# Turning x one element ahead, with the attention product and the low keys on POOL

## The reference

```python
qkv = x @ Wqkv + bqkv                       # q: 16 heads of 16; k, v: 4 groups of 16, tiled to 16 heads
scores = einsum('bqhd,bkhd->bhqk', q, k) / HD
out = einsum('bhqk,bkhd->bqhd', softmax(scores), v)
x1 = layernorm(x + out @ Wout + bout)
gate, up = split(x1 @ ternary_quant(w_gate_up).T)     # H = 1024
h = silu(gate) * up
y = layernorm(x1 + rms_norm(h) @ ternary_quant(w_proj).T)
```

## Time and profile before

| | |
|---|---|
| median of three runs | 575.34 us |
| profiled execution | 574.5 us, span 571.8 us |
| PE busy | 528.4 us, 92% |
| DVE busy | 455.4 us, 80% |
| ACT busy | 374.2 us, 65% |
| POOL busy | 319.5 us, 56% |
| mean granted clock of TensorE | 0.990 |

### The profile page before, as it was taken

How to read it: one execution, slowest core, us unless ns; L and a number is a source line. 1 busy time by engine, 2 the same in 40 slices (tenths; PEclk the granted TensorE clock), 3 DMA queues, 4 the chain that set the end, 5 groups by cost and what they waited for, 6 DMA issues and landing times.

```text
span 571.8 us, 13792 instructions
## 1 busy us (share of the span) xinstructions
PE 528.4 (92%) x4176; PEld 444.7 (78%) x4176; DVE 455.4 (80%) x1025; ACT 374.2 (65%) x754; POOL 319.5 (56%) x478
## 2 busy tenths in 40 slices
PE   6497999999999999999999999999999999999883
PEld 5386778778888787878888888878887877787772
DVE  6878877788888888888888887888898888885764
ACT  5456755666767767676776776776767676667663
POOL 5577671255645555555646564556555565466764
PEclk9899999999999999999999999999999999999998
DMA  7865444343333426062534444261606253010001
GB/s 229 144 142 95 86 95 104 74 91 88 84 95 93 105 68 128 19 160 26 128 69 102 93 94 100 79 116 56 134 6 166 29 125 71 12 44 6 19 20 37
DMA packets 53931, 49.05 MB, mean 86 GB/s; under 512 B 6144, under 2 KB 53888, under 8 KB 53888
## 3 DMA queue, kind: packets, MB, share of 16 engines
q1 hardware_dynamic: 53200, 48.13, 38.2%
q10 hardware_dynamic: 688, 0.39, 0.2%
HBM read 33.29 MB, written 14.68 MB: 84 GB/s over the span
## 4 chain that ended last, share of the span: by engine, by line
PE 63%; DVE 20%; issue 7%; POOL 4%; ACT 2%; DMA 2%; SPq 0%; DVEq 0%; ACTq 0%; POOLq 0%
PE ffn_ps L551 19%; PE short_ps L477 10%; PE pv_ps L579 8%; PE short_ps L523 8%; PE down_ps L564 7%; PE exp_ps L532 6%; DVE row_max L800 5%; DVE gated L863 3%; DVE h_f L870 3%; PE short_ps L587 2%; DVE attB L902 2%; DVE pvT L896 1%; DVE w_hat L833 1%; POOL sq_sum L966 1%; DVE w_sum L821 1%
## 5 line engine op out<-in xcount | busy, mean ns | idle before, releaser
L800 DVE TENSOR_REDUCE row_max<-short_ps 128x2 f32<-128x512 f32 x256 | 173.4, 681 | 67.2 <-PE short_ps L523 66.8
L961 POOL TENSOR_TENSOR h_lo<-h_f,h_hi 128x256 fp32r<-128x256 f32 x128 | 94.8, 740 | 206.9 <-ACT h_hi L698 206.8
L722 ACT ACTIVATE probs<-exp_ps 128x1024 f32<-128x1024 f32 x128 | 130.7, 1021 | 34.1 <-PE exp_ps L532 33.2
L523 PE MATMUL short_ps<-k_st,q_st 65*128 65x256 f32 x512 | 108.2, 294 | 9.3 <-DVE v_ones L919 6.2
L523 PEld LDWEIGHTS short_ps<-k_st,q_st 65*128 65x128 f32 x512 | 87.9, 192 | 20.7 <-issue 7.8
L707 ACT ACTIVATE tanh<-ffn_ps 128x256 f32<-128x256 f32 x120 | 45.5, 380 | 85.2 <-PE ffn_ps L551 85.2
L551 PE MATMUL ffn_ps<-x1T_hi,wguT 128*128 128x256 f32 x480 | 82.0, 293 | 10.3 <-DVE h_f L870 8.9
L564 PE MATMUL down_ps<-wpT,h_hi 128*128 128x256 f32 x256 | 78.7, 330 | 3.8 <-POOL h_lo L961 3.8
L532 PE MATMUL exp_ps<-q_st,k_st 67*128 67x512 f32 x256 | 80.7, 397 | 0.8 <-DMA q_st<-shift_lo 0.6
L551 PEld LDWEIGHTS ffn_ps<-x1T_hi,wguT 128*128 128x128 f32 x480 | 64.8, 189 | 19.3 <-issue 9.7
L966 POOL TENSOR_TENSOR sq_sum<-sq_sum,h_sq 128x256 f32<-128x256 f32 x105 | 79.5, 758 | 0.0
(11 more groups left out here) (102 smaller groups left out, 830.7 us busy)
## 6 DMA issues: line engine op xcount, KB each, us to landing
q_st<-q_dram SPq DMA_DIRECT2D x128, 128.0 KB, 4.1
q_dram<-q_p SPq DMA_DIRECT2D x16, 512.0 KB, 3.0
xn<-in_L_attn_x_dram SPq DMA_DIRECT2D x16, 256.0 KB, 3.4
k_st<-k_dram SPq DMA_DIRECT2D x64, 64.0 KB, 2.8
res<-in_L_attn_x_dram SPq DMA_DIRECT2D x16, 256.0 KB, 2.9
out_dram<-y_out SPq DMA_DIRECT2D x16, 256.0 KB, 2.9
wgu_raw<-in_L_ffn_w_gate_up_dram SPq DMA_DIRECT2D x8, 256.0 KB, 6.6
k_dram<-k_p SPq DMA_DIRECT2D x16, 128.0 KB, 2.4
```

The source lines that it names most:

```text
L523: last = pe.matmul(bank[:, t * S:(t + 1) * S], q_st[0:PAD, st.par, head, t * P:(t + 1) * P], k_st[0:PAD, st.par, st.s % 4, :], start=True, ...
L722: act.activation(probs[:, st.s % 4], exp_ps[:], ACT.Exp).then_inc(exp_done, 1)
L800: dve.tensor_reduce(row_max[:, st.par, head * TT:(head + 1) * TT], short(n, f"max{i}")[:].rearrange("p (t k) -> p t k", t=TT), AX.X, ALU.m ...
L961: pool.tensor_tensor(h_p[1][:, st.s % 4, :], h_f[:, st.s % 2, :], h_p[0][:, st.s % 4, :].bitcast(F32), ALU.subtract).then_inc(h_lo, 1)
```

## The change

Four things are changed.

- **x**: it is loaded one element earlier (`LOAD_X = -8`) and turned at offset -2, that is in slot 6 of the element before, ahead of `down` and not behind it, and ACT's copy of it stands in slot 6 too. It uses bank `short2` and not `short0`. Element 0 is still turned in slot 1, element 1 in slot 6 of the ramp.
- **Attention product**: for elements 2 to 14 the multiplication (`attB`) is done by POOL, one slot later (slots 5 and 1) and first in POOL's slot; DVE's turning of it (`attT`) stands at the end of the same slots.
- **Low part of k**: from element 3 on POOL computes it, in slot 4, ahead of the second layer norm's small steps.
- **Identity products**: in slot 8 of the ramp PE does 18 more of them, behind a wait on the first piece's eviction (`w_ev`).

The loop starts at slot 72 and makes three passes instead of four.

```diff
-LOAD_X = 0
-X_T = 1
+LOAD_X = -8
+X_T = -2
+FIRST_X_T = 1
...
+PV_BACK = (21, 25)
...
-X_HIGH = 1
...
-              1: {"max0": 0, "max1": 2, "x": 0, "shift1": 1},
+              1: {"max0": 0, "max1": 2, "shift1": 1},
...
-              6: {"max0": 0, "max1": 1},
+              6: {"max0": 0, "max1": 1, "x": 2},
...
+CLOCK_WAIT, CLOCK_LONG = 8, 18
...
-LOOP_FROM, BODY = 64, 2 * SLOTS
+LOOP_FROM, BODY = 72, 2 * SLOTS
...
+def x_turn(n):
+
+    if n.it is None and n.t == FIRST_X_T:
+        return Step(0, 0, None)
+    st = n.once(X_T)
+    return st if st and (st.it is not None or st.b) else None
...
+def product_on_pool(st):
+
+    return st.it is not None or 2 <= st.b < B - 1
+
+
+def low_keys_on_pool(st):
+
+    return st.it is not None or st.b >= 3
...
+        def normalised(eng):
+            return eng.tensor_tensor(
+                attB[:].rearrange("p (b g d) -> p g b d", b=NB, g=2),
+                pvT[:].rearrange("p (g b e) -> p g b e", g=2, b=NB)[:, :, :, 0:HD],
+                den_r[:].rearrange("p (g b) -> p g b", g=2).unsqueeze(3).broadcast_to([P, 2, NB, HD]),
+                ALU.mult).then_inc(att_done, 1)
...
@@ block.tensor, slot
                 keep_clock(n, 2)
+                if st := x_turn(n):
+                    bank = short_ps[BANK[X_T % SLOTS, "x"]] if st.it is None and st.b == 0 else use_short(n, "x")
+                    if st.it is None and st.b == 1:
+                        pe.wait_ge(k_copied, 1)
+                    wait(pe, x_loaded[st.par], st.count2(16, 16))
+                    turn(bank, [xn[:, st.par, t, k * P:(k + 1) * P] for k in range(DT) for t in range(TT)], xT_made)
                 if st := n.chunk(DOWN0):
                     down(st)
-                if st := n.once(X_T):
-                    bank = use_short(n, "x")
-                    wait(pe, x_loaded[st.par], st.count2(16, 16))
-                    turn(bank, [xn[:, st.par, t, k * P:(k + 1) * P] for k in range(DT) for t in range(TT)], xT_made)
                 if (c := turned_piece(n, 0)) is not None:
                     turn_weights(c)
+                if n.it is None and n.t == CLOCK_WAIT:
+                    pe.wait_ge(w_ev, 1)
+                    for _ in range(CLOCK_LONG):
+                        pe.matmul(turn_banks[0][:, 0, 0:P], ident[:], ident[:], start=True, stop=True)
...
@@ block.scalar, slot
-                if st := n.once(X_HIGH):
+                if st := x_turn(n):
                     wait(act, xT_made, st.count(1, 1))
                     wait(act, k_made, st.count(1, 0))
                     high(xT[:], both(n, "x")).then_inc(xT_copied, 1)
...
@@ block.vector
+            def turn_attention(st, half):
+
+                wait(dve, att_done, st.count(2, half + 1))
+                wait(dve, o_made, st.count(1, 0))
+                dve.transpose(attT[:, half, :], attB[:]).then_inc(att_turned, 1)
...
-                        wait(dve, den_done, st.count(2, half + 1))
-                        wait(dve, att_turned, st.count(2, half))
-                        dve.tensor_tensor(
-                            attB[:].rearrange("p (b g d) -> p g b d", b=NB, g=2),
...
-                        wait(dve, att_done, st.count(2, half + 1))
-                        wait(dve, o_made, st.count(1, 0))
-                        dve.transpose(attT[:, half, :], attB[:]).then_inc(att_turned, 1)
-                if st := keys(n):
+                        if not product_on_pool(st):
+                            wait(dve, den_done, st.count(2, half + 1))
+                            wait(dve, att_turned, st.count(2, half))
+                            normalised(dve)
+                            turn_attention(st, half)
+                    if (st := n.once(PV_BACK[half])) and product_on_pool(st):
+                        turn_attention(st, half)
+                if (st := keys(n)) and not low_keys_on_pool(st):
                     wait(dve, k_copied, st.count(1, 1))
                     low(k_p[:, 1, :], kv_f[0:KV, :], k_p[:, 0, :]).then_inc(k_lo, 1)
...
@@ block.gpsimd
             def slot(n):
+                for half in range(2):
+                    if (st := n.once(PV_BACK[half])) and product_on_pool(st):
+                        wait(pool, den_done, st.count(2, half + 1))
+                        wait(pool, att_turned, st.count(2, half))
+                        normalised(pool)
...
+                if (st := keys(n)) and low_keys_on_pool(st):
+                    wait(pool, k_copied, st.count(1, 1))
+                    pool.tensor_tensor(k_p[:, 1, :], kv_f[0:KV, :], k_p[:, 0, :].bitcast(F32), ALU.subtract
+                                       ).then_inc(k_lo, 1)
```

More of the change, by code:

```diff
@@ L302, in short @@
             if name == "k" and n.it is None and n.t == PROJ_Q:
-                return short_ps[BANK[X_T, "x"]]
+                return short_ps[BANK[X_T % SLOTS, "x"]]
             return short_ps[BANK[SHORT_OFFSET.get(name, n.t) % SLOTS, name]]
@@ L899, in slot @@
                                        ).then_inc(den_done, 1)
-                        wait(dve, den_done, st.count(2, half + 1))
-                        wait(dve, att_turned, st.count(2, half))
-                        dve.tensor_tensor(
-                            attB[:].rearrange("p (b g d) -> p g b d", b=NB, g=2),
-                            pvT[:].rearrange("p (g b e) -> p g b e", g=2, b=NB)[:, :, :, 0:HD],
-                            den_r[:].rearrange("p (g b) -> p g b", g=2).unsqueeze(3).broadcast_to([P, 2, NB, HD]),
-                            ALU.mult).then_inc(att_done, 1)
-                        wait(dve, att_done, st.count(2, half + 1))
-                        wait(dve, o_made, st.count(1, 0))
-                        dve.transpose(attT[:, half, :], attB[:]).then_inc(att_turned, 1)
-                if st := keys(n):
+                        if not product_on_pool(st):
[6 more added lines that the diff above has]
+                if (st := keys(n)) and not low_keys_on_pool(st):
                     wait(dve, k_copied, st.count(1, 1))
```

## The result

The changed kernel takes **593.04 us** (median of 4 executions, 589.98 to 594.42) against 575.35 us before: ratio 1.0306, 95% interval 1.0283 to 1.0329. Slower was right, 583.7 us and the range up to 590 were not: the loss is 17.7 us and not 8.4. The profiled execution took 593.23 us with a span of 591.3 us, 19.5 us more than before's.

A forecast was written before the change was run, and what follows sets the result against it. PE's in-order work, plus two places per element where DVE is late, was taken as the bound. From 574.5 us, -5.2 + 14.2 + 0.4 + 0 - 1 = +8.4 gave 582.9, as median 583.7 us; own range 579 to 587, wider 578 to 590.

The forecast's parts named there:

- Slot 1, -0.43 us each: Slot 1 without x's four turns: 0.43 us shorter in each of 12 steady slots, -5.2 us in all.
- The wait in slot 6 and its +1.29 us: Slot 6: x's turns wait for `x1T_lo`, slot 7's max0 comes 1.29 us later; +14.2 us over 11 elements.
- Product and keys on POOL, 0: Slots 4 to 6: slot 6's DVE times stay as they were, 0; bounds -3 to +6 us for 11 elements.
- DVE's gain is used up in that wait: Slots 4 to 6: DVE's freed 0.79 and 0.47 us are lost as `attT` waits for POOL before slot 6's row maximum.
- the bound of -3: Faster bound for product and low keys on POOL: -0.3 us an element if the product takes 0.42 us.
- The ramp, -1: Ramp, 20.50 to 31.00 us: added products and turns fill PE's hole and raise the clock; -1 us, bounds 0 and -2.5.
- The clock: Rival: PE stands about 2 us in each element, clock falls to 0.50, 2.15 us each, 607 us; chance 0.02.
- Hole filled: Rival, slot 6: `x1T_lo` read before x's turns, which then fit the hole before `h_f`; about 568.8 us, chance 0.09.

## Why the prediction was wrong

Point by point:

- *Slot 1, -0.43 us each.* Right: 3.59 us where it was 4.02. Its condition was right too, that DVE also loses the product from slot 0: with x's move alone the gain is 0.15 us at most.
- *The wait in slot 6 and its +1.29 us.* Mechanism right: the turns stand behind max1 and wait for `x1T_lo`, with a hole of 1.46 to 1.60 us. Where the clock holds, slots 6 to 7 take 1.4 to 1.5 us more (4.56 against 3.15, 4.70 against 3.22).
- *Product and keys on POOL, 0.* The durations were near (product 0.62 against 0.7 taken, keys 0.73 against 0.7), and so was the wait of `attT` for `attB`. The step that failed here is the sentence that DVE's gain is used up in that wait. Slot 6's row maximum came 1.94 us after the turns of x1 (2.18 before), because gate and up of slot 6 no longer wait for `h_f`, and what PE gains at the start of slot 6 stays. That is 0.35 to 0.4 us less in each element; alone it makes the kernel 4 to 5 us faster, beyond the bound of -3.
- *The ramp, -1.* Wrong in sign, by the count: 18 products are 36 instructions and 5.9 us, which end behind the wait. The change is 2.3 us faster without them, and the kernel before is 3.1 us slower with them. The clock behind them was near 1 as foretold (0.97) and gave nothing back in total, since the maxima started 2 us later.
- *The clock.* This is the step that put the time out of the range. The fall in each element was a rival with 0.02, argued away by the 1.00 of a stretch whose holes are half a microsecond, though the sum itself had just made a hole three times as long. Behind 6 of the 11 holes PE fell to 0.50, at 1.5 us each and 3.0 for the long one. The trace after has 10.6 us of it, and the experiment that fills the holes gives 11.0 us back. What the Trainium skill describes in the section cited there ("TensorE: Matmul & The Clock Gate", "HAM oscillation — how this bites in real kernels"), a clock lost again in every turn of a loop with waits, was the better guide. The trace agrees with it in kind only: the waits of the page's example are longer than these holes, and here not every turn lost the clock.

The sum with measured sizes, for the span of the profiled execution: the eleven elements cost 0.6 us each, 6.7 in all, and not 0.86 and 9.5 as forecast (POOL's 0.4 is the main difference); the clock adds 10.6, the start 2.2, and what follows the eleven nothing: 19.5 us.

"Hole filled" was priced at 568.8 us. The version whose x doesn't meet `x1T_lo` takes 570.16 us with the 18 products, 569.01 us with v moved too, and 566.59 us with 8 products and v moved: what kept the change from it was a bank, not DVE's time.

## What to carry to other kernels

Before an instruction goes to another slot of an in-order engine, ask which buffer it takes there and who reads that buffer last; the choice of banks alone decided here between -0.9% and +3.1%, with the same 18 products in both. A new hole on TensorE has two prices, its length and what the clock loses behind it; if the hole is longer than any in the trace, the trace's full clock says nothing for it. A gain in one slot can need two things to leave it at once. Work that fills a wait should be counted in instructions and set to end before the wait does, and useful work that is ready (`down` here) is a better filling than none.

## What the chip showed that was not expected

- Equal holes have unequal results. In the changed kernel the clock fell behind six of the seven holes of 1.53 or 1.54 us, and behind none of the four others, three of them 1.60 us long and one 1.46. From the hole at 197.05 us on it was exactly every second one. Without the identity products it fell behind 7, one of 1.46 us among them, and with the product on DVE behind 3 of the 8 holes of 1.46 us and none of the 3 of 1.53 or 1.54. So between 1.46 and 1.60 us the length doesn't decide, and what does is open.
- Twelve useless instructions in each element (1.60 us of PE's time) made the kernel 1.9% faster.
- The product with a broadcast operand takes 0.62 us on POOL and 0.44 us (median, before) on DVE; beside POOL's work DVE's took up to 0.79 us. The low keys on 64 partitions take 0.73 us on POOL, as long as a row of 128 partitions (`h_lo`, 0.74 us).
